# A first stage with its angles in turns, shorter table arithmetic, half of the z pairs summed, and late wo blocks spread over the loop

## The reference

```python
# token mixing: K[c,h,l] for 64 batches c, 128 tokens h, 1024 positions l
dt_Lambda = dt[:, None] * Lambda                   # 128 tokens x 64 complex poles
Wc = W * (exp(dL) - 1) * reciprocal((exp(dL * 1024) - 1) * Lam, 1e-7)
K  = einsum('chn,hnl->chl', Wc, exp(dt_Lambda[..., None] * pos - P_max)).real
# attention: 32 heads, 8 kv heads, rotary, causal softmax
h = K + attn(layernorm(K), Wq, Wk, Wv, Wo)
# feed-forward of 8 low-rank experts, softmax router
h = h + ffn(layernorm(h), A, B, Wr, br)
```

## Time and profile before

| | us |
|---|---|
| median of 3 executions | 2368.4 |
| lowest and highest | 2367.73, 2368.97 |
| the profiled execution, its own time | 2369.94 |
| its span, first to last instruction | 2368.1 |
| busy in the span: TensorE | 2259.8 (95%) |
| VectorE | 1889.4 (80%) |
| ScalarE | 1840.5 (78%) |
| GpSimd | 1710.4 (72%) |

### The profile page before, as it was taken

The page is one execution under the profiler, slowest core; times in us unless marked ns, Lnnn a source line. Parts: engine busy times, 40 slices in busy tenths (PEclk is TensorE's granted clock), DMA queues, the critical chain, the costliest instruction groups (busy, mean ns, idle before and its releaser), DMA issues.

```text
span 2368.1 us, 58968 instructions
## 1 busy us (share of the span) xinstructions
PE 2259.8 (95%) x18704; PEld 1250.6 (53%) x18704; DVE 1889.4 (80%) x7794; ACT 1840.5 (78%) x6301; POOL 1710.4 (72%) x1529
## 2 busy tenths in 40 slices
PE   3998689999999999999999999999999999999986
PEld 2787245555555555555555555555555555555543
DVE  8999568788788887878878878888787887887864
ACT  7998478777887777787777788777778777778872
POOL 2544288787787777777778778777777777877871
PEclk9999899999999999999999999999999999999987
DMA  3888488899899999998999999998999998998983
GB/s 99 265 242 267 125 146 171 177 175 173 173 176 167 176 175 172 176 175 169 173 174 175 173 174 177 166 176 173 174 176 175 172 167 176 175 173 174 169 151 83
DMA packets 1192387, 410.10 MB, mean 173 GB/s; under 512 B 1150598, under 2 KB 1152902, under 8 KB 1192076
## 3 DMA queue, kind: packets, MB, share of 16 engines
q1 hardware_dynamic: 1192072, 406.33, 86.8%
q10 hardware_dynamic: 4, 0.00, 0.0%
HBM read 53.84 MB, written 67.11 MB: 51 GB/s over the span
## 4 chain that ended last, share of the span: by engine, by line
PE 85%; DVE 1%; ACT 1%; DMA 1%; POOL 1%; issue 0%; SPq 0%; POOLq 0%; DVEq 0%; ACTq 0%
PE pb L956 14%; PE pa L956 14%; PE pc L956 14%; PE s_ps L969 5%; PE pa L943 5%; PE pa L942 5%; PE pa L944 5%; PE pb L942 5%; PE pb L944 5%; PE pb L943 5%; PE pv_ps L987 2%; PE pd L987 2%; PE pd L942 1%; PE pd L944 1%; PE pd L943 1%; ACT pr L1110 1%
## 5 line engine op out<-in xcount | busy, mean ns | idle before, releaser
L1110 ACT ACTIVATE pr<-pr,smin 128x128 f32<-128x128 f32 x2048 | 793.1, 389 | 182.9 <-DVE smin L1256 182.7
L1475 POOL TENSOR_TENSOR pr<-pr,rinv 128x512 f32<-128x512 f32 x512 | 577.0, 1137 | 422.8 <-DVE rinv L1264 412.4
L1483 POOL TENSOR_TENSOR p<-pr,p 128x512 f16<-128x512 f32 x512 | 590.9, 1158 | 13.0 <-ACT p L1120 5.4
L1256 DVE CUSTOM_DVE_ANT_0 pr<-s_ps,cst 128x128 f32<-128x128 f32 x2048 | 468.8, 286 | 97.4 <-PE s_ps L969 59.3
L1120 ACT ACTIVATE p<-pr 128x512 f16<-128x512 f32 x512 | 318.8, 623 | 160.7 <-POOL pr L1475 137.3
L1110 ACT ACTIVATION_READ_ACCUMULATOR pr<-pr,smin 128x1 f32 x2048 | 384.3, 188 | 0.0
L956 PE MATMUL pa<-wkv_hi,xt 128*128 128x512 f16 x1024 | 326.5, 380 | 23.7 <-DMA xt<-xs 23.7
L956 PE MATMUL pb<-wq_hi,xt 128*128 128x512 f16 x1024 | 326.8, 380 | 1.2 <-DVE rows L1374 1.2
L956 PE MATMUL pc<-wq_hi,xt 128*128 128x512 f16 x1024 | 324.8, 379 | 0.0
L694 PE MATMUL hps<-z,xw 128*128 128x256 f32 x848 | 188.8, 383 | 50.0 <-POOL xw L381 36.2
L969 PE MATMUL s_ps<-kt,qt 128*128 128x128 f16 x2048 | 199.0, 220 | 9.4 <-DVE smin L1256 5.1
(11 more groups left out here) (203 smaller groups left out, 4897.3 us busy)
## 6 DMA issues: line engine op xcount, KB each, us to landing
h<-rows SPq DMA_DIRECT2D x128, 256.0 KB, 3.6
out<-rows SPq DMA_DIRECT2D x64, 512.0 KB, 2.9
rows_in<-h SPq DMA_DIRECT2D x38, 512.0 KB, 4.5
h_ln<-h SPq DMA_DIRECT2D x25, 512.0 KB, 4.4
pt<-p SPq DMA_TRANSPOSE x512, 3.6
xa<-x SPq DMA_DIRECT2D x16, 256.0 KB, 3.9
xb<-x SPq DMA_DIRECT2D x32, 128.0 KB, 3.6
wst<-wq SPq DMA_DIRECT2D x8, 512.0 KB, 5.5
```

The costliest lines, as they stand in the source:

```text
L1110: last = A.activation(p, p, ACT.Exp, bias=smin[g % 2][:, j:j + 1], scale=-1.0, accum_out=rsum[g % 2][:, j:j + 1])
L1256: V.tensor_tensor_reduce(pr[g % 2][:, cols], s_ps[g % 2][:, cols], mask, 1.0, 3e38, ALU.add, ALU.min, smin[g % 2][:, j:j + 1]).then_inc(ma ...
L1475: nc.gpsimd.tensor_tensor(p3, p3, rinv[g % 2][:, :].unsqueeze(2).broadcast_to([P, HG, P]), ALU.mult).then_inc(p_norm, 1)
L1483: nc.gpsimd.tensor_tensor(p[:, HG * P:], pr[g % 2][:, :], p[:, 0:HG * P], ALU.subtract).then_inc(pl_done, 1)
```

## The change

- **Angles in turns.** The imaginary rate lam is multiplied by 1/(2 pi) once (in two parts, `lam_t`), so theta counts turns. Bringing it into range is then two operations (round by adding and subtracting MAGIC in one operation, subtract) in place of five. The scale goes into ScalarE's Sin. The same for the 6 x 128 elements ahead of the loop.
- **Negative cosine and sine tables.** The sine of the half angle is scaled by sqrt(2) before it is squared, so half is 2 sin squared of the half angle, and the real table is (half - 1) * expo in one operation in place of two; the sine comes out negative by a negative scale.
- **One sum of z a step.** Every odd pair is summed, and pair 62: 33 of 64 pairs in place of 22; in chunk 7 five in place of eight.
- **Late wo blocks over the loop.** Block 2 is an ordinary piece (window 10). Blocks 3 to 7 are loaded in windows 13, 17, 21, 25 and 28, in place of six from 24 to 29; memory: expo's quarters in the order in which they come free, and h_ln1. tab[0] isn't used for it.
- **Rows back.** Tokens 0 to 95 are read back in window 26, 96 to 111 in window 29, in place of 0 to 111 in window 29.
- **FEW = 6**: 6 columns of expo before the first sines in place of 16.

```diff
@@ -57,17 +57,16 @@
 XWR = 4
 LEAD = 3
 ON_ACT = 3
-EARLY = 112
-EARLY_AT = WINDOWS - 3
-FIRST_ROWS = 16 * (2 + 3 * 2)
-LATE = (2, 3, 4, 5, 6, 7)
-LATE_LOADED = (24, 27, 27, 28, 29, 29)
-LATE_HIGH = {WINDOWS - 3: (0, 1), WINDOWS - 2: (2, None), WINDOWS - 1: (3, 4), WINDOWS: (5,)}
+EARLY = {WINDOWS - 6: (0, 96), WINDOWS - 3: (96, 112)}
+FIRST_ROWS = 16 * (3 + 3 * 2)
+LATE = (3, 4, 5, 6, 7)
+LATE_LOADED = (13, 17, 21, 25, 28)
+LATE_HIGH = {WINDOWS - 3: (0, 1), WINDOWS - 2: (2, None), WINDOWS - 1: (3, None), WINDOWS: (4,)}
 MAGIC = 12582912.0
-INV_2PI = 0.15915494309189535
-TWO_PI_HI = 6.28125
-TWO_PI_LO = 2.0 * float(np.pi) - 6.28125
+INV_2PI_HI = float(np.float32(0.15915494309189535))
+INV_2PI_LO = 0.15915494309189535 - INV_2PI_HI
 PI_SAFE = 3.1415925
+SQRT_2 = 2.0 ** 0.5
 
 
 C_IDENT, C_MASK = 0, 128
@@ -136,7 +135,8 @@
         layer_stage(nc, h0, out, W, h_sent, ln_in)
 
 
-V_X, V_F, V_T, N_PRE = 10, 16, 23, 46
+V_X, V_F, V_T, N_PRE = 12, 15, 22, 45
+FEW = 6
 A_TAU, A_HALF, A_HY, A_EXPO, A_TOP = 2, 4, 6, 7, 8
 
 
@@ -172,6 +172,7 @@
         top_r = sb("top_r", [P, TOPS, T])
 
         lam_p = sb("lam_p", [P, 2])
+        lam_t = sb("lam_t", [P, 1])
         gt0 = sb("gt0", [P, 1])
         sgn = sb("sgn", [P, 1])
         off = sb("off", [P, 2])
@@ -209,8 +210,8 @@
 
 
         grown = expo[:, :, :].rearrange("p t n -> p (t n)").rearrange("p (i d) -> p i d", i=4)
-        late = [W["h_ln1"][:, :], grown[:, 0, :], grown[:, 1, :], grown[:, 2, :],
-                tab[0][:, :, :, :].rearrange("p t s n -> p (t s n)"), grown[:, 3, :]]
+        late = [grown[:, 0, :], grown[:, 1, :], grown[:, 2, :], W["h_ln1"][:, :], grown[:, 3, :]]
+        last_grown = {0: 1, 1: 3, 2: 5, 4: 7}
 
         hps = [ps(f"hps{i}") for i in range(4)]
         u = [ps(f"u{i}") for i in range(2)]
@@ -239,11 +240,10 @@
         tok_done = sem("tok_done")
         h_copied = sem("h_copied")
 
-        TV, TA, TP = 10, 3, 3
-        SUM_AT = (1, 3)
+        TV, TA, TP = 6, 3, 3
 
         def summed(g):
-            return g // (TC // 2) == CHUNKS - 1 or g % 2 == 1 and g // 2 % PER_CHUNK in SUM_AT
+            return g == T // 2 - 2 or g % 2 == 1
 
         def sums_before(g):
             return sum(summed(n) for n in range(g))
@@ -312,11 +312,9 @@
                         at += piece.shape[1]
 
                 def load_late(i):
-                    if i == 1:
-                        sp.wait_ge(tab_v, TV * (CHUNKS - 1) + 7)
-                        sp.wait_ge(tab_p, TP * (CHUNKS - 1) + 2)
-                    if i == 4:
-                        sp.wait_ge(z_made, (CHUNKS - 1) * TC // 2)
+                    if i in last_grown:
+                        sp.wait_ge(tab_v, TV * last_grown[i] + 3)
+                        sp.wait_ge(tab_p, TP * last_grown[i] + 2)
                     sp.dma_start(late[i], wo[LATE[i] * P:LATE[i] * P + P, :]).then_inc(late_in[i], 16)
 
                 def sent(g):
@@ -363,11 +361,11 @@
                             load_late(i)
                     if w < WINDOWS - 1:
                         store(2 * w + 1)
-                    if w == EARLY_AT:
-                        rows_back(0, EARLY)
+                    if w in EARLY:
+                        rows_back(*EARLY[w])
                     if w == WINDOWS - 2:
                         first_rows(T // 2 - 3)
-                        rows_back(EARLY, T - 6)
+                        rows_back(T - 16, T - 6)
                 first_rows(T // 2 - 2)
                 sp.wait_ge(h_copied, T)
                 sp.dma_start(*first_of(T // 2 - 1, 1)).then_inc(ln_in[0], 16)
@@ -389,14 +387,14 @@
                         if at in (0, 2, 3) and lows:
                             pool.wait_ge(w_lo, lows)
                         if at == 0:
-                            pool.wait_ge(tab_v, TV * k + 10)
+                            pool.wait_ge(tab_v, TV * k + 6)
                             first_angles(nc.gpsimd, k + 1).then_inc(tab_p, 1)
                         if at == 2:
                             pool.wait_ge(tab_a, TA * (k + 1) + 2)
                             pool.wait_ge(z_made, k * (TC // 2))
                             table_i(nc.gpsimd, k + 1).then_inc(tab_p, 1)
                         if at == 3:
-                            pool.wait_ge(tab_v, TV * (k + 1) + 7)
+                            pool.wait_ge(tab_v, TV * (k + 1) + 3)
                             pool.wait_ge(tab_p, TP * (k + 1) + 2)
                             digits_m1(nc.gpsimd, k + 1).then_inc(tab_p, 1)
                     add(w)
@@ -406,11 +404,11 @@
                 A = nc.scalar
 
                 def sines(k):
-                    act.wait_ge(tab_v, TV * k + 5)
-                    A.activation(half[:, :, :], theta[:, :, :], ACT.Sin, scale=0.5).then_inc(tab_a, 1)
+                    act.wait_ge(tab_v, TV * k + 2)
+                    A.activation(half[:, :, :], theta[:, :, :], ACT.Sin, scale=PI_SAFE).then_inc(tab_a, 1)
                     act.wait_ge(tab_a, TA * k + 1)
-                    A.activation(theta[:, :, :], theta[:, :, :], ACT.Sin).then_inc(tab_a, 1)
-                    A.activation(half[:, :, :], half[:, :, :], ACT.Square).then_inc(tab_a, 1)
+                    A.activation(theta[:, :, :], theta[:, :, :], ACT.Sin, scale=-2.0 * PI_SAFE).then_inc(tab_a, 1)
+                    A.activation(half[:, :, :], half[:, :, :], ACT.Square, scale=SQRT_2).then_inc(tab_a, 1)
 
                 def products(w, e):
                     q, slot = w // 2, w // 2 % XR
@@ -449,15 +447,15 @@
                 act.wait_ge(pre_v, V_X)
                 A.activation(tau, xr[:, 0:2, :], ACT.Tanh, scale=0.5).then_inc(pre_a, 1)
                 A.activation(mag, xr[:, 2:LENGTHS, :], ACT.Exp).then_inc(pre_a, 1)
-                for n in range(DIG):
+                for n in range(FEW):
                     growth(n)
                 act.wait_ge(pre_v, V_F)
-                A.activation(hy, pf, ACT.Sin, scale=0.5).then_inc(pre_a, 1)
-                A.activation(sy, pf, ACT.Sin).then_inc(pre_a, 1)
+                A.activation(hy, pf, ACT.Sin, scale=PI_SAFE).then_inc(pre_a, 1)
+                A.activation(sy, pf, ACT.Sin, scale=2.0 * PI_SAFE).then_inc(pre_a, 1)
                 act.wait_ge(pre_a, A_HALF)
                 A.activation(hy, hy, ACT.Square).then_inc(pre_a, 1)
                 sines(0)
-                for n in range(DIG, NPOS - 1):
+                for n in range(FEW, NPOS - 1):
                     growth(n)
                 growth(NPOS - 1).then_inc(pre_a, 1)
                 act.wait_ge(pre_v, V_T)
@@ -499,37 +497,26 @@
                     if k == 0:
                         first_angles(V, k).then_inc(tab_p, 1)
                     dve.wait_ge(tab_p, TP * k + 1)
-                    V.tensor_scalar(turns[:, :, :], theta[:, :, :], INV_2PI, MAGIC, ALU.mult, ALU.add).then_inc(tab_v, 1)
+                    V.tensor_scalar(turns[:, :, :], theta[:, :, :], MAGIC, MAGIC, ALU.add, ALU.subtract).then_inc(tab_v, 1)
                     dve.wait_ge(tab_v, TV * k + 1)
-                    V.tensor_scalar(turns[:, :, :], turns[:, :, :], MAGIC, None, ALU.subtract).then_inc(tab_v, 1)
-                    dve.wait_ge(tab_v, TV * k + 2)
-                    V.scalar_tensor_tensor(theta[:, :, :], turns[:, :, :], -TWO_PI_HI, theta[:, :, :],
-                                           ALU.mult, ALU.add).then_inc(tab_v, 1)
-                    dve.wait_ge(tab_v, TV * k + 3)
-                    V.scalar_tensor_tensor(theta[:, :, :], turns[:, :, :], -TWO_PI_LO, theta[:, :, :],
-                                           ALU.mult, ALU.add).then_inc(tab_v, 1)
-                    dve.wait_ge(tab_v, TV * k + 4)
-                    V.tensor_scalar(theta[:, :, :], theta[:, :, :], PI_SAFE, -PI_SAFE,
-                                    ALU.min, ALU.max).then_inc(tab_v, 1)
+                    V.tensor_tensor(theta[:, :, :], theta[:, :, :], turns[:, :, :], ALU.subtract).then_inc(tab_v, 1)
 
                 def tables(k):
                     dve.wait_ge(tab_a, TA * k + 3)
                     dve.wait_ge(pre_a, A_EXPO)
-                    V.tensor_scalar(half[:, :, :], half[:, :, :], -2.0, 1.0, ALU.mult, ALU.add).then_inc(tab_v, 1)
                     if k == 0:
                         table_i(V, k).then_inc(tab_p, 1)
-                    dve.wait_ge(tab_v, TV * k + 6)
-                    V.tensor_tensor(tab[k % 2][:, :, 0, :], expo[:, k * TC:k * TC + TC, :], half[:, :, :],
-                                    ALU.mult).then_inc(tab_v, 1)
+                    V.scalar_tensor_tensor(tab[k % 2][:, :, 0, :], half[:, :, :], -1.0,
+                                           expo[:, k * TC:k * TC + TC, :], ALU.add, ALU.mult).then_inc(tab_v, 1)
 
                 def digits(k):
                     m1, m2 = (a[:, :, :].rearrange("p t (s n) -> p t s n", s=2) for a in (dm1, dm2))
-                    dve.wait_ge(tab_v, TV * k + 7)
+                    dve.wait_ge(tab_v, TV * k + 3)
```

(21 more changed lines are left out.)

## The result

The changed kernel takes 2354.64 us, the median of 4 executions (2350.41 to 2355.52), against 2368.68 of the kernel before on the same chip (4 executions, 2367.73 to 2369.98). The ratio is 0.994, with a 95% interval of 0.9928 to 0.9953: faster by 14.0 us, where 17.9 were forecast. The profiled execution took 2353.86 us, its span is 2352.1, and the granted clock was 0.986 on average.

What follows compares the result with a forecast made beforehand. TensorE was taken to lead a steady chunk (24.39 of 24.75 us busy), VectorE and ScalarE close behind. Terms -2.5 - 1.2 - 1.4 + 0.2 - 6.9 - 6.1 = -17.9 us gave 2350.5 us, range 2346 to 2360.

Steps and rivals of the forecast that it cites:

- VectorE's price list: Steady chunk on VectorE: angles 2.92 to 1.07 us, tables 1.25 to 0.61, two more sums 1.6; together -0.9.
- The start: Before the first product: shorter VectorE chain, ten expo columns moved behind the sines; -2.5 us, bounds -2.2 and -3.5.
- Window 0: Chunk 1's angles behind GpSimd's second addition: one operation left instead of three, 1.83 us to 0.65; -1.2 us.
- The second and third chunk: Second loses 0.9 and a 0.42 us wait for wo_hi: -1.4; third loses 0.9, gains wo block 2's 1.15: +0.2.
- The steady chunks: Four chunks from 24.75 to 23.05 us each, VectorE becoming the bound; -6.9 us, bounds -4.0 and -7.6.
- Slower: Rival: late loads delay both following stores, h buffers pass it on, each costing several waits; 2385 us at two each; chance 0.03.
- The last chunk: End of the first stage: one pair in two summed in three windows, 34.2 us to 28.1; -6.1 us, bounds -3, -7.
- The hand-over: From the first stage's end at 248.07 to the layer's first product at 259.17: stays, no change.
- The DMA engines with some waits: Rival, steady part: share near 0.94, one 3.4 us wait per late load, +13.6, 2364 us; half, 2357; chance 0.14.
- ScalarE is the bound: Rival, steady chunks: ScalarE's work sets a 23.75 us period; 2354.5 us; chance 0.18.
- The hand-over eats it: Rival: layer's start hangs on stores or rows, losing all but the first 3.7 us; 2364.7 at worst; chance 0.05.
- Queues: SyncE's queue: one late 512 KB load in windows 13, 17, 21, 25, 28; changed issue counts take no time in themselves.

Runs made afterwards that it cites:

- changed_again: The changed kernel run once more, unaltered, to see the noise between two profiles; 2354.43 us (0.9944).
- late_old: Changed kernel with six late wo blocks again, loaded in windows 24, 27, 27, 28, 29 and 29 as before; 2351.96 us (0.9933).
- late_small: Changed kernel with only 16 of 128 rows loaded of late wo blocks 3, 4 and 5; 2352.14 us (0.9933).
- late_even: Changed kernel with late wo loads in windows 14, 18, 22, 26 instead of 13, 17, 21, 25; 2352.26 us (0.9937).
- few16: Changed kernel with 16 instead of 6 columns of expo ahead of the first sines; 2355.78 us (0.9952).
- new_sums_alone: Kernel before the change with only the new choice of summed pairs (odd pairs and pair 62); 2366.75 us (0.999).
- old_sums: Changed kernel with the pairs summed as before: two of eight in chunks 0 to 6, all in chunk 7; 2364.55 us (0.9983).
- late_quarters: low_early with each late load cut into four 128 KB pieces, in windows 12 to 27 one a window behind the second store; 2355.01 us (0.9945).
- low_early: late_even with the low halves of three late blocks put ahead of the last window's ordinary ones on VectorE; 2351.03 us (0.9926).

## Why the prediction came out as it did

The direction and the engine that becomes the bound (VectorE) came as forecast, and five of the seven steps within 0.7 us. Up to the layer's first product 13.6 us came where 17.9 were forecast; the medians differ by 14.0, with the layer's own variation of some microseconds over it. One term is wrong by 4.1 us; the forecast stayed near because the rest of the sum held.

- **VectorE's price list held.** Angles 1.05 us (forecast 1.07), fused table 0.60 from start to start (0.61), sums 0.76. The unheld chunk is 22.87 to 22.89 us where 23.05 was taken: the small waits went too, which the forecast gave as its other value, 22.9.
- **TensorE at 0.2205 us a record held**, at 96 records a chunk (96 × 0.2205 is 21.2, it was busy 21.4 to 21.5 where nothing held it), and at the end of the stage: 205.7 to 228.07 is 22.3 us, 22.2 were forecast.
- **The start: -2.7**, with the chain as forecast: ScalarE's columns are what VectorE waits for, 1.51 us at 26.04 (25.2 to 26.2 forecast). The table load shows as an instruction of 1.28 us, where the forecast read it as a gap of 1.3.
- **Window 0: -1.6 to window 4's addition** instead of -1.2 (-1.0 in changed_again, so the forecast lies inside what executions differ by), although the first operation with immediates, L500, took 2.58 us at 35.63, 0.1 more than its like in the earlier trace rows.
- **The second and third chunk: -1.1 and +0.3**, against -1.4 and +0.2. late_old splits the third: without block 2 it is 24.02 us, 0.9 less than before, and block 2 adds 1.25 (the forecast has 0.9 and 1.15).
- **The steady chunks: -2.8 instead of -6.9.** This is the term that was mis-sized, by 4.1 us, and nearly the whole miss. The forecast wrote "So VectorE becomes the bound, with cover of a few tenths" and "Behind each stands the store of the window's second pair, whose landing frees a buffer for an eviction two pairs later", so it named the place, and put nothing into its sum for it. The reason it gave under "Slower", that stores landed in 3.5 us with the same loads of wq in the stream, is a median over all stores: the two directly behind each wq took 4.8 to 5.2 us before the change (steady part), and with a second 512 KB ahead of them they took 5.7 to 6.6. The first of the four chunks is free of waits: the first late load was issued only at 126.13. The three behind it have one eviction each that waits, 2.21 us at 134.41, 1.53 at 158.97 and 1.82 at 183.23, and lose 1.4 to 1.7 us each (24.24 to 24.58 less 22.87). The third of these waits the profile puts down to TensorE, but it ends 0.08 us behind the store's landing like the others, and in changed_again the same one, 2.12 us at 183.25, has the store. ScalarE's cover of some tenths means that a wait of an eviction goes through almost whole: eviction, wq_hi, wq_lo, z, TensorE, as the lines at 134.41, 144.12 and 148.05 show. In changed_again 0.5 us of each wait is absorbed (1.86, 1.99 and 2.12 against 1.30, 1.54 and 1.64 lost), which is the cover. late_small takes three of the loads away, and the loss goes; late_even moves them, and most of it goes.
- **The last chunk: -5.0 instead of -6.1.** The evictions still waited for stores: 2.17 us at 223.05 was the longest, where the kernel before has 3.41 in the earlier trace rows and 3.72 at 227.44. One of those waits, 1.58 us at 207.24, is behind the late load of window 25. The bound of -3 "if the evictions still wait for stores once" was too pessimistic: one wait does not cost 3 us.
- **The hand-over: -0.7** instead of nothing (-0.4 in changed_again). Why is not known.

Of the rivals, the one with chance 0.14, "The DMA engines with some waits", named the right event and the right number, one wait for each of the four late loads of the steady part, with too high a price: 1.5 to 2.2 us rather than 3.4. Its reason, a full share, is not the cause: the held chunks stand at 0.86 to 0.88, and late_even runs nearly unheld at 0.90 to 0.92. The argument against it was wrong as well: 62.9 to 89.6 ran at 267 GB/s without a wait, but an average over a chunk says nothing about what stands directly ahead of a store. The DMA view over the steady part (40 slices of 2.5 us, 105 to 205 us) shows peaks of 406 GB/s next to slices of 180, and a median landing of the stores above the 3.5 us of the earlier trace rows. Neither is the cause: late_even, nearly unheld, has a slice of 391 and a median of 4.0. The changed kernel:

```profile
GB/s 192 264 363 283 222 279 262 189 218 184 350 406 312 227 225 276 262 179 238 226 374 376 265 243 230 265 279 168 236 263 394 372 246 257 234 294 278 117 269 279
...
h<-rows SPq DMA_DIRECT2D x67, 256.0 KB, 3.9
```

That the Trainium skill ("DMA: Bandwidth & Descriptors", "Specifications") gives about 358 GB/s to a core from HBM did not help: slices here show 406, loads and stores together, and the waits came in chunks with means of 268 to 271.

"ScalarE is the bound" is refuted as it was put: in late_small it has 22.5 to 22.6 us of work in chunks of 22.89 and holds nobody. The sign that the forecast gave for it, VectorE waiting for wq_hi longer than 0.3 us every fourth window, did appear (1.57 us at 144.12), but ScalarE was late there because its eviction had waited for a store, which was the sign for the DMA rival. What it does is pass on what it has waited for. The rivals "Slower" and "The hand-over eats it" did not occur: no load cost more than one wait in the steady part. The forecast's count of the issues under "Queues" is off (six late loads became five and one ordinary piece), and nothing in its sum hangs on it.

GpSimd and VectorE: the sum L558 that now stands in window 0 ran while GpSimd's second addition did:

```profile
35.02 0.68 DVE L558 TENSOR_TENSOR z<-z 128x512 f32<-128x512 f32 x1
35.63 2.58 DVE L500 TENSOR_SCALAR turns<-theta 128x512 f32<-128x512 f32 x1
...
35.25 2.67 POOL L379 TENSOR_TENSOR xw<-xw,pi 128x1024 f32<-128x1024 f32 x1 [0.79 <-DVE xw L537]
```

The addition took 2.67 us, and 2.67 and 2.66 in few16 and new_sums_alone, while the sum kept its 0.68 us. In the kernel before and in old_sums, where no sum stands there, the same addition takes 2.40. This is the exclusion that the Trainium skill describes in "SBUF — State Buffer", "SBUF: two separate sides", for a VectorE operation with two SBUF inputs: the one that came second gave way, here the addition, by 0.3 us. In old_sums VectorE comes second, with the subtraction L502 of two tensors at 35.60, 0.23 us behind the addition's start, and takes 2.72 us instead of 0.69. In the steady chunks VectorE comes second too, by a little: a sum begins 0.2 us before the end of an addition and takes 0.76 us, where the one in window 0 takes 0.68. So the 0.76 of the price list had it in already, at some 0.08 us a sum.

*What stays open.* That two loads of 512 KB one behind the other, directly ahead of stores, cost the steady part its 4.7 us is shown, by the landings and by late_small. What is not settled is the rest: why the even windows still cost 1 to 2.7 us over the four chunks, with waits that differ between executions that issue the same; and why quarters cost up to 2.3 us a chunk (25.20 less 22.87) although no load of theirs is larger than 128 KB. The stores that hold up late_quarters were issued behind wq or behind x; whether it is the quarter beside them that makes them late was not tried.

## What to carry to other kernels

When two engines stand within a microsecond of each other, a change that relieves one is worth little until the other is relieved as well (-1.6 and -3.8 us alone, -14.0 together); price both, and then ask for the third, whose cover has become the smallest. A load that "costs no time" can be paid by whatever is issued behind it on its queue: look at which stores stand behind it and how long those took, not at the median of all, and at the slack of the engine that waits for them, not at the mean GB/s. Keep two large loads apart. Of the layouts tried, low_early has the lowest median, 2351.03 us (0.9926, 0.9912 to 0.9941), against the changed kernel's 2354.43 to 2354.64 (0.9928 to 0.9956 over both). The intervals overlap, but its first product stands 4.6 us earlier in the profile. It can't be told from late_even (2352.26) or late_old (2351.96).

## What was unexpected of the hardware

- Stores of 256 KB landed in 3.9 us (median) in the steady part against 3.5 before, and the longest took 6.6 instead of 5.3 us. Only the second number is tied to the loss: late_even has a median of 4.0, a longest of 5.8, and chunks some 1 us shorter at a higher load of the DMA engines.
- The last part of an unchanged stage had a granted clock of 0.72, 0.76 and 0.84 in three profiles (before, changed, new_sums_alone), and the stage took 2108.9, 2106.5 and 2104.4 us. The ten others lie between 2106.4 and 2108.2 at 0.74 to 0.77. The interval of a median of four is 6 us wide here; that this is a good part of it is likely but not shown. The place where a first-stage change ends is read much more sharply than its time.
- GpSimd's addition was longer by 0.3 us when a VectorE addition of two SBUF operands began 0.23 us before it. An operation with two immediates on VectorE, 0.41 us alone, took 2.58 us beside that addition, to 0.3 us behind its end, and in old_sums a subtraction of two tensors, 0.69 us alone, took 2.72 beside it.
